# A conv-attention-MoE block on one core: one merged weight for the scores in place of separate query and key projections

## The reference, cut to what matters

```
h = group_norm(x, gn_scale, gn_bias)            # B=4, C=128, T=1024
q = Wq^T h + bq ; k = Wk^T h + bk ; v = Wv^T h + bv
w = softmax over keys of (q^T k) * C**-0.5
x = x + (Wp^T (w v) + bp)
...                                             # linear attention, then the experts
```

## Time and profile before

| | |
|---|---|
| runs | 334.31, 334.0, 335.09 us (median 334.31) |
| profiled execution | 334.79 us, of which the span from first to last instruction is 332.9 us |
| PE busy | 301.8 us (91%) |
| DVE busy | 256.0 us (77%) |
| ACT busy | 191.8 us (58%) |
| POOL busy | 102.1 us (31%) |
| granted TensorE clock | 1.000 mean over the span |

### The profile page before, as it was taken

The page is one execution under the profiler, slowest core; times in us unless marked ns, Lnnn a source line. Parts: engine busy times, 40 slices in busy tenths (PEclk is TensorE's granted clock), DMA queues, the critical chain, the costliest instruction groups (busy, mean ns, idle before and its releaser), DMA issues.

```text
span 332.9 us, 5172 instructions
## 1 busy us (share of the span) xinstructions
PE 301.8 (91%) x1569; PEld 235.6 (71%) x1569; DVE 256.0 (77%) x623; ACT 191.8 (58%) x332; POOL 102.1 (31%) x154
## 2 busy tenths in 40 slices
PE   2887989989989899789989996999999997999995
PEld 2776868777968677577768785867757774666884
DVE  4799686678686798987687885787688685777995
ACT  3356474676570586445277656458567435856883
POOL 2345350059102664500636200089120037000000
PEclk9999999999999999999999999999999999999999
DMA  5902000010000011000000106396520692239511
GB/s 152 300 0 66 0 1 2 0 66 0 0 3 0 0 65 64 2 12 0 0 1 0 63 12 201 132 376 255 172 91 0 177 372 112 71 116 385 189 33 63
DMA packets 12757, 29.58 MB, mean 89 GB/s; under 512 B 2192, under 2 KB 5952, under 8 KB 10816
## 3 DMA queue, kind: packets, MB, share of 16 engines
q1 hardware_dynamic: 12448, 29.00, 25.3%
q10 hardware_dynamic: 288, 0.33, 0.3%
HBM read 24.73 MB, written 4.59 MB: 88 GB/s over the span
## 4 chain that ended last, share of the span: by engine, by line
PE 59%; DVE 23%; issue 7%; ACT 4%; DMA 3%; POOL 2%; SPq 1%; DVEq 0%; POOLq 0%; ACTq 0%
PE ring L1403 7%; PE ring L1721 6%; PE ring L1405 6%; PE ring L1404 6%; PE ring L1418 6%; PE scores L1403 6%; PE scores L1405 6%; PE scores L1404 6%; DVE prob L1019 4%; DVE pT_lo L1026 4%; PE ring L1555 2%; DVE lst L1056 2%; ACT prob L674 2%; PE ring L1533 2%; DVE t L1045 1%
## 5 line engine op out<-in xcount | busy, mean ns | idle before, releaser
L819 ACT ACTIVATE gel<-scores,b_c 128x512 f32<-128x512 f32 x64 | 43.9, 688 | 35.6 <-PE scores L1405 32.5
L1019 DVE TENSOR_SCALAR_CACHE_REDUCE prob<-scores 128x1024 f32<-128x1024 f32 x32 | 38.9, 1215 | 12.1 <-PE scores L1405 12.0
L1026 DVE TENSOR_TENSOR pT_lo<-ring,pT_hi 128x512 fp32r<-128x512 f32 x64 | 40.7, 681 | 8.1 <-ACT pT_hi L680 7.6
L556 POOL TENSOR_SCALAR rstd<-lmv 128x8 f32<-128x8 f32 x8 | 2.1, 260 | 135.3 <-DVE lmv L1062 135.3
L680 ACT ACTIVATE pT_hi<-ring 128x512 fp32r<-128x512 f32 x64 | 34.3, 598 | 14.5 <-PE ring L1418 14.5
L674 ACT ACTIVATE prob<-prob,row_max 128x1024 f32<-128x1024 f32 x32 | 36.8, 1151 | 9.5 <-DVE prob L1019 9.3
L1418 PE MATMUL ring<-ident,prob 128*128 128x128 f32 x256 | 33.9, 276 | 8.2 <-ACT prob L674 5.8
L1418 PEld LDWEIGHTS ring<-ident,prob 128*128 128x128 f32 x256 | 28.4, 140 | 14.0 <-ACT prob L674 6.1
L1403 PE MATMUL scores<-wT_hi,w_hi 128*128 128x512 f32 x64 | 34.2, 534 | 0.0
L1403 PE MATMUL scores<-k_both,q_hi 128*128 128x512 f32 x64 | 27.3, 427 | 0.9 <-DVE k_both L1004 0.9
L1403 PE MATMUL ring<-pT_hi,v_hi 128*128 128x512 f32 x64 | 26.7, 417 | 1.2 <-DVE pT_lo L1026 1.2
(11 more groups left out here) (297 smaller groups left out, 725.9 us busy)
## 6 DMA issues: line engine op xcount, KB each, us to landing
pT_hi<-scratch_s SPq DMA_DIRECT2D x8, 1024.0 KB, 6.6
prob<-scratch_s SPq DMA_DIRECT2D x4, 1024.0 KB, 7.7
k_both<-scratch_s SPq DMA_DIRECT2D x3, 1024.0 KB, 6.7
z_in<-scratch_z SPq DMA_DIRECT2D x8, 256.0 KB, 3.2
out_dram<-out_s SPq DMA_DIRECT2D x8, 256.0 KB, 2.2
xb<-in_x_dram SPq DMA_DIRECT2D x3, 512.0 KB, 3.1
scratch_z<-out_s SPq DMA_DIRECT2D x2, 512.0 KB, 2.8
k_both<-scratch_s SPq DMA_DIRECT2D x4, 256.0 KB, 4.4
```

The source lines that it names most:

```text
L819: act.activation(half(gel, s % 2), scores[:, s % 2, :], ACT.Gelu, bias=b1_c[:, s % E:s % E + 1]).then_inc(e_gelu, 1)
L1019: dve.tensor_scalar(prob[:, i % 2, :], scores[:, 2 * (i % 2):2 * (i % 2) + 2, :].rearrange("p a t -> p (a t)"), -1.0, None, ALU.mult, ALU. ...
L1026: dve.tensor_tensor(tile_group(pT_lo, n, i), as_tiles(ps(place, unit)), tile_group(pT_hi, n, i).bitcast(FP32), ALU.subtract).then_inc(drai ...
```

## The change

The scores are rewritten. With M = Wq Wk^T (made once from the two weights, which are first turned on PE), the queries are projected with -C**-0.5 times M, the bias of the queries goes through Wk, and the keys are h itself (for batch 0, x itself, with the group norm's factor on both sides of M). The key bias gives a term that depends on the row alone: h times a column. It is made by 8 FP32 matmuls of one column per batch (unit `kb`), taken out by ACT into `key_bias`, and added by DVE in `row_maximum`, whose immediate factor of -1 becomes the addition of a column read from SBUF. The units k0 and k1 and all their work are gone.

The high and low parts of h are now keys for the whole batch, so they get two buffers (`h_both[:, b % 2]`), and the hardware loops of all engines are written out. `first_norm` (h_f of batch 0) ran twice and runs once. The order of several steps changes, and so do the bank tables. The core of the diff, long but cut:

```diff
-SETUP_UNITS = dict(gn_mean=0, gn_var=1, bias_qk=2)
+SETUP_UNITS = dict(turned=0, gn_mean=1, merged=2, gn_var=3, scaled=0, biases=1, bias_qk=2, bias_s=3)
-SECOND_UNITS = dict(T6a=0, T6b=1, q0=2, T7a=3, T7b=0, k0=1, k1=2, q1=3, PV1=0, OT1=0, v0=1, v1=2, T0a=3,
+SECOND_UNITS = dict(T6a=1, T6b=2, q0=3, T7a=0, T7b=1, q1=2, kb=3, PV1=0, OT1=2, v0=1, v1=2, T0a=3, T0b=0,
-LOOP_UNITS = dict(T6a=2, T6b=3, ctx=0, q0=1, T7a=2, T7b=3, m2=0, k0=1, k1=2, m3=3, q1=0, PV1=1, o0=2, o1=3,
-                  OT1=1, v0=0, v1=1, T0a=2, T0b=3, T1a=0, T1b=1, xT0=2, xT1=3, w0=0, w1=1, T2a=2, T2b=3,
+LOOP_UNITS = dict(T6a=2, T6b=3, ctx=0, q0=1, T7a=2, T7b=3, m2=0, q1=1, kb=2, m3=3, PV1=0, o0=1, o1=2, OT1=2,
+                  v0=3, v1=0, T0a=1, T0b=2, T1a=3, T1b=0, xT0=1, xT1=2, w0=3, w1=0, T2a=1, T2b=2, lg0=3,
...
# ACT, start
-            split_first()
-            act.wait_ge(ld_w["cols"], 64)
-            act.activation(bqs_c, bq_c, ACT.Copy, scale=SCALE).then_inc(bqs_made, 1)
+            take_setup("turned", qk_turned)
+            split_first(0)
+            take_setup("merged", merged_both)
+            split_first(1)
...
# ACT, opening_batch
-                project(place, "q0", q_hi, bqs_c)
-                project(place, "k0", k_hi, bk_c)
-                project(place, "k1", k_hi, bk_c)
-                project(place, "q1", q_hi, bqs_c)
+                project(place, "q0")
+                project(place, "q1")
+                take_key_bias(place)
                 softmax(b, 0)
+                project_v(place)
                 softmax(b, 1)
-                project_v(place)
...
# DVE, first_weights
-                dve.tensor_scalar(wq_sc, wq_raw, SCALE, g, ALU.mult, ALU.mult)
-                dve.tensor_scalar(wq_hi[:, :], wq_raw, SCALE, g, ALU.mult, ALU.mult)
+                dve.tensor_scalar(gn_diag, ident[:, :], g, -SCALE, ALU.mult, ALU.mult).then_inc(diag_made, 1)
...
+                wait_filled(dve, SETUP, "scaled")
+                scaled = tile(ps(SETUP, "scaled"), 0)
+                after(dve.tensor_scalar(wm_hi[:, :], scaled, g, None, ALU.mult))
+                dve.scalar_tensor_tensor(out=wm_lo[:, :], in0=scaled, scalar=g, in1=wm_hi[:, :].bitcast(FP32),
+                                         op0=ALU.mult, op1=ALU.subtract).then_inc(setup_made, 1)
...
# DVE, row_maximum
+                if i == 0:
+                    wait_drained(dve, place, "kb")
                 dve.wait_ge(s_made, b * TILES + i + 1)
                 dve.tensor_scalar(prob[:, i % 2, :],
                                   scores[:, 2 * (i % 2):2 * (i % 2) + 2, :].rearrange("p a t -> p (a t)"),
-                                  -1.0, None, ALU.mult, ALU.min, accum_out=row_max[:, i:i + 1]).then_inc(s_max, 1)
+                                  key_bias[:, i:i + 1], None, ALU.add, ALU.min, accum_out=row_max[:, i:i + 1]).then_inc(s_max, 1)
...
# DVE, opening_batch
+                project(place, b, "q0")
+                project(place, b, "q1")
+                first_norm()
                 take(place, "wvT", wvT[:, :])
-                first_norm()
-                group_stats(1)
                 row_maximum(place, b, 0)
                 merge_weights()
+                group_stats(1)
                 row_maximum(place, b, 1)
+                project_v(place, b)
                 group_stats(2)
-                project_v(place, b)
                 turn_probs(place, b, 0)
...
# DVE, batch
                 residual(place, la, 1)
+                norm1_half(place, la, 0)
                 project_v(place, b)
                 turn_probs(place, b, 0)
                 row_maximum(place, b, 2)
-                norm1_half(place, la, 0)
                 norm1_half(place, la, 1)
...
# PE, start (const_made, then)
+            turn(SETUP, "turned", [wq_raw, wk_raw])
+            group_means(SETUP, 0, 0, 1)
+            wait_drained(pe, SETUP, "turned")
+            dst = open_unit(SETUP, "merged")
+            pe.matmul(dst[:, 0:C], wqT, wkT, start=True, stop=True)
+            fill(SETUP, "merged", pe.matmul(dst[:, C:2 * C], wkT, wqT, start=True, stop=True))
+            group_variances(SETUP, 0, 0, 1)
             first_biases()
+            keep_busy(5)
+            wait_drained(pe, SETUP, "merged")
+            pe.wait_ge(diag_made, 1)
+            small(SETUP, "scaled", C, mergedT, gn_diag)
+            rest_of_biases()
...
+            def take_key_bias(place):
...
+                dst = open_unit(place, "kb")
+                src, bias = (xb, bias_first) if place is FIRST else (h_f, bias_rest)
+                for i in range(TILES):
+                    last = pe.matmul(dst[:, i:i + 1], tile(src, i), bias[:, 1:2], start=True, stop=True)
+                fill(place, "kb", last)
...
# PE, opening_batch
-                project(place, b, "q0", wq_hi, wq_lo)
-                project(place, b, "k0", wk_hi, wk_lo)
-                project(place, b, "k1", wk_hi, wk_lo)
-                project(place, b, "q1", wq_hi, wq_lo)
+                project(place, b, "q0")
+                project(place, b, "q1")
+                first_constant()
+                take_key_bias(place)
+                wait_drained(pe, place, "q0")
+                score(b, 0)
                 pe.wait_ge(ld_w["wv"], 16)
                 turn(place, "wvT", [wv_s[:, :]])
-                for unit in ("q0", "k0", "k1"):
-                    wait_drained(pe, place, unit)
-                score(b, 0)
                 wait_drained(pe, place, "wvT")
                 pe.wait_ge(ld_w["wp"], 16)
                 small(place, "wpv", C, wvT[:, :], wp_s[:, :])
-                pe.wait_ge(ld_w["cols"], 64)
                 small(place, "bias_o", 1, wp_s[:, :], bv_c)
-                score(b, 1)
                 wait_drained(pe, place, "wpv")
                 pe.wait_ge(h_f_made, 1)
                 project_v(place)
+                score(b, 1)
                 turn_probs(place, b, 0)
...
                 group_variances(place, 2, 1, B - 1)
+                biases_again(place)
                 attend(place, 0, 0, 2)
...
# PE, batch
-                project(place, b, "k0", wk_hi, wk_lo)
-                project(place, b, "k1", wk_hi, wk_lo)
+                project(place, b, "q1")
+                take_key_bias(place)
                 if lc is not None:
                     merge3(place)
-                project(place, b, "q1", wq_hi, wq_lo)
                 attend(place, 1, 0, 2)
...
-            with pe.Fori(2, B) as b:
+            for b in range(2, B):
                 batch(loop_place(b), b, b - 1, b - 2)
```

More of the change, by code:

```diff
@@ L238, in conv_attention_moe @@
         lgT = p1[0:E, :]
-        hs_hi = [m[:, n * BANK:(n + 1) * BANK] for m in (h_hi, q_hi) for n in range(2)]
-        hs_lo = [m[:, n * BANK:(n + 1) * BANK] for m in (h_lo, q_lo) for n in range(2)]
+        hs_hi = [m[:, n * BANK:(n + 1) * BANK] for m in (h_both[:, 0, 0, :], q_hi) for n in range(2)]
+        hs_lo = [m[:, n * BANK:(n + 1) * BANK] for m in (h_both[:, 0, 1, :], q_lo) for n in range(2)]
         hs_hi += [pT_lo[:, n, :] for n in range(HELD - 4)]
@@ L345, in apart, with h_parts @@
             eng.sem_inc(passed[eng], 1)
+        def h_parts(b, n):
+            return [h_both[:, b % 2, k, n * BANK:(n + 1) * BANK] for k in range(2)]
         def tile(m, j):
@@ L433, in _ @@
             load_x(2)
-            with sp.Fori(2, B - 1) as b:
+            for b in range(2, B - 1):
                 load_x(b + 1)
@@ new lines, in first_weights, with first_biases @@
+                dve.sem_inc(drained[SETUP.bank("scaled")], 1)
+            def first_biases():
+                wait_filled(dve, SETUP, "biases")
+                both = ps(SETUP, "biases")
+                after(dve.tensor_copy(bias_first[:, 0:2], both[:, 0:2]))
+                after(dve.tensor_tensor(bias_first[:, 0:2], both[:, 2:4], bias_first[:, 0:2], ALU.add))
+                after(dve.tensor_scalar(bias_first[:, 0:2], bias_first[:, 0:2], gmul[:, 0:1], -SCALE, ALU.mult, ALU.mult))
+                dve.sem_inc(drained[SETUP.bank("biases")], 1)
+                dve.sem_inc(bias_made, 2)
@@ L963, in _ @@
+                dve.sem_inc(drained[FIRST.bank("again")], 1)
+                dve.sem_inc(bias_made, 1)
             dve.memset(rt_hi[:, :].bitcast(FP32), 0.0)
@@ L1267, in batch @@
                     route_b()
+                key_sums(place, la)
+                if lc is not None:
                     route_c()
-                key_sums(place, la)
                 turn_probs(place, b, 4)
@@ L1281, in _ @@
             batch(SECOND, 1, 0, None)
-            with dve.Fori(2, B) as b:
+            for b in range(2, B):
                 batch(loop_place(b), b, b - 1, b - 2)
@@ L1457, in project, with take_key_bias @@
                 pe.wait_ge(h_lo_made, b * HALVES + n + 1)
-                whole(place, unit, (hi[:, :], lo[:, :]), (half(h_hi, n), half(h_lo, n)))
+                whole(place, unit, (wm_hi[:, :], wm_lo[:, :]), h_parts(b, n))
+            def take_key_bias(place):
```

(10 more changed lines are left out.)

175 lines of the change are left out of this document (90 added, 85 removed).

## The result

The changed kernel takes 346.34 us (median of 4, 344.24 to 349.15), the kernel before 334.15 beside it (333.57 to 335.09): ratio 1.0364, 95% interval 1.0329 to 1.0400. The direction was forecast, the size was not: +12.2 us against +2.0, and the time is outside the range of 332.6 to 338.4. The profiled execution is the longest of the four, 349.15 us with a span of 347.1; its mean granted clock is 0.979, against 1.000 before. All four executions of the changed kernel have 0.970 to 0.980, those of the kernel before, here and beside the experiments, 0.993 to 1.000. An execution counts as slow when it is over 1.5% above the fastest of its kernel; the only two such are of kb_opening_only.

What follows compares the result with a forecast made beforehand. The bound was taken to alternate between PE (busy 91% of the span) and DVE. The terms 3.1 + 0.2 + 0.7 - 1.1 - 1.3 + 0.4 = +2.0 us gave a median of 336.3 us, 8-in-10 range 332.6 to 338.4.

Steps and rivals of the forecast that it cites:

- The hole of batches 2 and 3: DVE's 1.28 us wait for ACT's v_hi; closing it was to gain 1.3 us per batch, less 0.2 in batch 2.
- The price of the products: Eight one-column key-bias products per batch on PE, bound by weight loads at 0.22 us each: 1.7 us.
- Rival 2: Key-bias products cost only 0.66 us, each batch gains 1.0 us on PE, result 332.1 us; chance 0.21.
- The start of batch 0: Opening, largest term: later setup, score 0 and row maximum 1 delay DVE's T0 by 3.1 us (+1.3 to +3.9).
- two projections instead of four end at about 15.0: Opening on PE: q projections start at 13.35 instead of 11.04 us, yet end at about 15.0 as before.
- 1.7 us more: Opening on PE: the key bias adds 1.7 us ahead of score 0, which starts at about 17.7 instead of 16.37.
- lasts 1.86 us: Opening on PE: v starts at 21.2 us, lasts 1.86, then score 1; row maximum 1 starts at 24.5.
- rival 3: PE's clock rises early, at 10.5 us; the opening loses 1.3 us less, result 335.0 us; chance 0.10.
- the pass of the maximum: DVE's 32 row-maximum passes read a column instead of a constant, 0.06 us each: +0.4 us (0 to +1.9).
- About half of them where DVE is late: Of 32 row-maximum passes, costing 1.9 us more in all, about half were taken to count.
- half again: Second halving for row-maximum passes, since the priced row reads SBUF and this pass PSUM; gave +0.4 us.
- Batch 1: +0.3 us key bias and +0.4 for PE's v waiting on residual through OT1's bank: +0.7 us (0 to +1.5).

Runs made afterwards that it cites:

- kb_opening_only: Changed kernel with the key-bias products in batch 0 only, batches 1 to 3 reusing its column: 340.08 us, ratio 1.0182.
- before_with_columns: Kernel before plus eight FP32 one-column products per batch ahead of q1, result overwritten: 341.14 us, ratio 1.0252.
- no_kb_constant: Changed kernel without the row term, the pass of the maximum multiplying by a constant again: 336.21 us, ratio 1.0057.
- wide_in_place_of_kb: Changed kernel with its eight one-column products per batch replaced by eight 512-column FP32R matmuls: 344.12 us, ratio 1.0287.
- kb_after_score0: Changed kernel with the opening's first_constant and key-bias products moved behind score 0: 346.09 us, ratio 1.0367.
- wide_after_score0: kb_after_score0 with batch 0's eight one-column products replaced by 512-column matmuls, batches 1 to 3 unchanged: 344.94 us, ratio 1.0318.
- no_kb_all: Changed kernel without row term, with batch 0's old order and setup edits, DVE's old T3 and key_sums order, own bank for batch 1's OT1: 333.24 us.
- the filler: no_kb_all plus seven unread 512-column matmuls in PE's 2.02 us pause of batch 2: 332.31 us, ratio 0.9956.
- before_with_wide: Kernel before plus eight 512-column FP32R matmuls per batch ahead of q1, result overwritten: 341.28 us, ratio 1.0200.

## Why the prediction was wrong

**Right.** `gmul` at 10.21 (forecast 10.8), q0 at 13.22 (13.35): the setup was followed well. The hole of batches 2 and 3 is closed, -1.1 us each (-1.3 and -1.3 without the key bias); DVE of the changed kernel runs from row maximum 1 of batch 2 to v_lo without a wait, where it had 1.28 us:

```profile
122.37 1.28 DVE L1048 TENSOR_SCALAR_CACHE_REDUCE prob<-scores,key_bias 128x1024 f32<-128x1024 f32 x1 [2.73 <-PE scores L1431]
...
123.58 1.12 DVE L1074 SCALAR_TENSOR_TENSOR t<-ring,row_sum,xT 128x128 f32<-128x128 f32 x4
124.73 0.87 DVE L1085 BATCH_NORM_STATS2 lst<-t 128x6 f32<-128x128 f32 x4
125.52 1.27 DVE L1023 TENSOR_TENSOR v_lo<-ring,v_hi 128x512 fp32r<-128x512 f32 x2
```

The price of the products was right where the clock is up: 1.70 us in batch 2 (108.45 to 110.15), and 6.9 us for four sets in before_with_columns. Rival 2, cheap products, is thereby out.

**The step that failed: "The start of batch 0".** It took PE's durations from the old trace as if the clock would be up from 13.8 us in the new one. Its "two projections instead of four end at about 15.0" ended at 15.94, its "1.7 us more" for the key bias were 3.4, "lasts 1.86 us" for v was 3.2: row maximum 1 came at 30.83, not 24.5. The clock had a place in the prediction only as rival 3, and there with the sign turned: it might come early. Some 3 us of the 15 are not the row term's: without it the clock rose at 17.0 (no_kb_constant), after both projections of the queries, which in the changed kernel too ran at the lower level throughout and so ended at 15.94. While the key-bias products ran, PE without a gap, it did not rise; with wide ones in their place it was up by their end, one profile each. The Trainium skill ("TensorE: Matmul & The Clock Gate", Part 1) says that activity releases the lower clock. The opening of wide_in_place_of_kb agrees. In kb_after_score0 and wide_after_score0 PE is busy with the eight products for equally long, and only the first has the stretch at 0.50 from 22.4 to 29.2 us. There the measurement decides.

**A cost that was not there: falls in mid-kernel.** No term and no rival had the granted clock fall again. The falls account for most of +1.8, +1.1 and +2.2 us in the table of stretches: where the same instructions met no fall, the stretches took 19.40 and 19.73 us instead of 21.02 and 21.33 (kb_after_score0), and without the row term the third took 26.96 instead of 28.24 (no_kb_constant). The falls come behind one-column products (opening of kb_after_score0; batches 2 and 3 of two of the four kernels that have them there) and behind pauses of PE of 1.66 and 2.02 us. The pause in front of T0 came with the new order; that of 2.02 us in batch 2 stayed in no_kb_all under DVE's old order. The first is supported by the pair with columns and wide matmuls, the second shown by the filler.

A pause of that length is not enough by itself, and not needed either. Of the ten profiles with the 2.02 us one, nine have a fall behind it (not no_kb_constant). All fourteen profiles have one of 1.64 us near 200 us, and none has a fall behind it; in the kernel before:

```profile
202.56 1.09 PE L1418 MATMUL ring<-ident,prob 128*128 128x128 f32 x8 [1.64 <-ACT prob L674]
```

The kernel before has only 1.29 and 1.12 us in batch 2 and no fall in its profile, but before_with_wide has the same two and falls at 148, and 11 of 66 executions of the kernel before have a clock of 0.993 to 0.995, as much as one stretch takes.

**A term mis-sized: the pass of the maximum.** "About half of them where DVE is late", then "half again", gave +0.4; the column costs 1.3 by the medians, inside the bounds of the term. The price of one pass was right (0.06 by the earlier trace rows; 0.060 measured); the second halving had no row behind it.

**Batch 1** cost +1.2 instead of +0.7. The forecast wait of v1 on the residual is there in the changed kernel, and with OT1 in a bank of its own (no_kb_all) the 16 products run as one:

```profile
74.55 1.16 PE L1528 MATMUL ring<-wpv,h_f 128*128 128x128 f32 x8 [1.19 <-DVE t L1074]
...
61.75 1.95 PE L1522 MATMUL ring<-wpv,h_f 128*128 128x128 f32 x16
```

Its price was not measured alone: the bank was one of three edits of no_kb_all, which gained 0.5 us in this stretch.

**The ladder**, each by its median: row term 8.8 us (346.3 to 337.5), column 1.3, order of batch 0 1.2, read-outs and filler 1.3, DVE's order and OT1's bank 0.5, the pause in batch 2 0.9. The steps of about 1 us are of the size of the intervals; by the ratios they are 1.5, 0.9, 1.1, 0.8 and 0.6. Of the 8.8, the kind of product accounts for about 2.2 (wide_in_place_of_kb). The rest I put down to the length, four times, at half the clock in the opening, and to `first_constant`, less what other engines' slack takes up; no run splits it.

**Open.** Why the columns of batches 2 and 3 bring the clock down in some profiles (the changed kernel, wide_after_score0) and not in others (before_with_columns, kb_after_score0), why the pause of 1.64 us near 200 us never does, and why the first rise comes at 13.4 us in one profile (kb_opening_only) and at 17 to 19 in others whose matmuls up to 15.9 us are the same. No run here tells it.

## What to carry to other kernels

Where a change makes the opening's PE work narrower, later or broken by pauses, don't carry durations over at the old clock: write down when matmuls change their distance, and give a late rise and a later fall a rival each with a price. A term that is constant along the softmax's axis should be dropped before it is made cheap; here that was worth 10 us. And a pause of PE of 2 us on a wait for DVE was in most executions followed by a fall that cost about 1 us; a little wide filler into a buffer that is overwritten anyway removed that. Look for the stretch of 0.50 before filling a pause, as others of nearly the same length had none.

## What the runs showed of the hardware

Eight FP32 products of one column, with PE busy in all that time, are followed by a granted clock of 0.50 in kb_after_score0, and eight 512-column FP32R matmuls of nearly the same length (1.93 against 1.79 us) are not. In the changed kernel the clock did not rise while such products ran at the lower level (17.50 to 20.91 us), nor in the six wide matmuls of score 0 behind them. A pause of PE of 2.02 us was followed by a fall in 9 of 10 profiles, one of 1.64 us near 200 us in 0 of 14. In the opening the granted-clock column reads 1.00 while equal matmuls are 0.43 us apart (score 0 of the changed kernel), so there the distance has to be read, not the column. The maximum over 128x1024 from PSUM takes 1277 ns with a column and 1217 with a constant.
